# A new order of the first microseconds: x ahead of half of W's second piece, and gamma and b_up spread behind the first half product

## The reference

```python
h = jnp.einsum('bsh,bhk->bsk', hidden_states, W_down[role]) + b_down[role][:, None, :]
h = jax.nn.gelu(h, approximate=False)
u = jnp.einsum('bsk,bkh->bsh', h, W_up[role]) + b_up[role][:, None, :]
y = hidden_states + u
mean = jnp.mean(y, axis=-1, keepdims=True)
var = jnp.mean(jnp.square(y - mean), axis=-1, keepdims=True)
yn = (y - mean) * jax.lax.rsqrt(var + LN_EPS)
return yn * gamma[role][:, None, :] + beta[role][:, None, :]
```

## Time and profile before

| | |
|---|---|
| median of 3 runs | 1417.29 us (1417.27 to 1417.34) |
| the profiled execution | 1416.96 us |
| its span | 1415.2 us |
| PE busy | 1401.1 us, 99% |
| DVE busy | 1204.8 us, 85% |
| ACT busy | 776.8 us, 55% |
| first product on PE | 12.17 us after the start of the span |

### The profile page before, as it was taken

One profiled execution on the slowest core, in us unless ns is written; L12 is line 12 of the kernel. 1 busy time (PEld: TensorE's weight loads), 2 busy tenths in 40 slices (PEclk: granted clock), 3 DMA queues, 4 the chain that ended last, 5 costly groups with the idle time before them and its releaser, 6 DMA issues.

```text
span 1415.2 us, 29331 instructions
## 1 busy us (share of the span) xinstructions
PE 1401.1 (99%) x6175; PEld 1158.2 (82%) x6176; DVE 1204.8 (85%) x1458; ACT 776.8 (55%) x2047; POOL 201.0 (14%) x300
## 2 busy tenths in 40 slices
PE   8999999999999999999999999999999999999997
PEld 6888888888888888888888888888888888888886
DVE  8798988888888888888888899988888888888887
ACT  5555555555555555555555555555555555555555
POOL 4376311100000000000000377311100000000000
PEclk9999999999999999999999999999999999999999
DMA  8677777766566666665666778777765666656654
GB/s 230 183 225 241 215 212 200 211 195 198 184 195 199 194 184 196 200 192 184 194 200 193 213 227 234 222 198 201 218 199 185 196 200 190 185 194 199 192 186 149
DMA packets 208868, 283.49 MB, mean 200 GB/s; under 512 B 25791, under 2 KB 155584, under 8 KB 208846
## 3 DMA queue, kind: packets, MB, share of 16 engines
q1 hardware_dynamic: 201438, 269.34, 61.4%
q0 software_dynamic: 5888, 12.07, 4.6%
q10 hardware_dynamic: 1520, 1.84, 0.4%
HBM read 183.27 MB, written 99.88 MB: 200 GB/s over the span
## 4 chain that ended last, share of the span: by engine, by line
PE 98%; DVE 1%; DMA 1%; issue 0%; ACT 0%; DVEq 0%; ACTq 0%
PE p_up L1120 16%; PE p_up L1118 16%; PE p_up L1119 16%; PE p_down L1118 16%; PE p_down L1120 16%; PE p_down L1119 16%; DMA row<-in_L_cond_W_down 0%; DMA x_quad<-in_x 0%; DVE row L1038 0%; PE p_hT L1114 0%; DVE row L866 0%; DMA w_raw<-in_itok_B 0%; DVE x_quad L820 0%; DVE wd_lo L758 0%; DVE x_quad L1024 0%
## 5 line engine op out<-in xcount | busy, mean ns | idle before, releaser
L1118 PE MATMUL p_down<-wd_hi,xT_hi 128*128 x1012 | 393.9, 389 | 0.7 <-DVE xT_lo L782 0.4
L1120 PE MATMUL p_down<-wd_hi,xT_lo 128*128 x1012 | 393.7, 389 | 0.0
L1119 PE MATMUL p_down<-wd_lo,xT_hi 128*128 x1012 | 393.7, 389 | 0.0
L1118 PE MATMUL p_up<-wu_hi,hT_hi 128*128 x1008 | 392.3, 389 | 0.0
L1120 PE MATMUL p_up<-wu_hi,hT_lo 128*128 x1008 | 392.1, 389 | 0.0
L1119 PE MATMUL p_up<-wu_lo,hT_hi 128*128 x1008 | 392.1, 389 | 0.0
L595 ACT ACTIVATE hT_hi<-p_hT 128x512 fp32r<-128x512 f32 x126 | 75.7, 601 | 381.5 <-DVE p_hT L800 378.9
L820 DVE SCALAR_TENSOR_TENSOR row<-p_up,row 128x1024 f32<-128x1024 f32 x126 | 154.2, 1224 | 126.3 <-PE p_up L1120 126.2
L581 ACT ACTIVATE xT_hi<-xT_raw 128x1024 fp32r<-128x1024 f32 x125 | 132.8, 1062 | 187.6 <-PE p_down L1120 185.6
L1118 PEld LDWEIGHTS p_down<-wd_hi,xT_hi 128*128 128x128 f32 x1012 | 189.6, 187 | 40.8 <-issue 1.4
L1119 PEld LDWEIGHTS p_down<-wd_lo,xT_hi 128*128 128x128 f32 x1012 | 190.3, 188 | 39.7
(11 more groups left out here) (174 smaller groups left out, 981.3 us busy)
## 6 DMA issues: line engine op xcount, KB each, us to landing
x_quad<-in_x SPq DMA_DIRECT2D x510, 128.0 KB, 3.4
row<-in_x SPq DMA_DIRECT2D x126, 512.0 KB, 4.0
out<-row SPq DMA_DIRECT2D x126, 512.0 KB, 2.7
h_dram<-h SPq DMA_DIRECT2D x125, 256.0 KB, 4.1
h_quad<-h_dram SPq DMA_DIRECT2D x498, 64.0 KB, 1.9
w_raw<-in_L_cond_W_down POOLq DMA_DIRECT2D x64, 64.0 KB, 3.2
w_raw<-in_L_cond_W_up POOLq DMA_DIRECT2D x64, 64.0 KB, 3.6
row<-in_L_cond_W_up SPq DMA_DIRECT2D x16, 128.0 KB, 3.6
```

Source lines behind the costliest of these rows:

```text
L1118: pe.matmul(dst, a_hi, w_hi, start=first, stop=False)
L1119: pe.matmul(dst, a_hi, w_lo, start=False, stop=False)
L1120: return pe.matmul(dst, a_lo, w_hi, start=False, stop=last)
```

## The change

In the order of the engines' functions:

- SP: one register load of four item numbers in place of two single ones. x of item 0 (quarters 0 and 1), then quarters 2 and 3 of W's piece 1, then x of item 1, then all of piece 2, then piece 3. Before: x of item 0 (0 and 1), x of item 1, half of piece 2, piece 3.
- ACT: issues only quarters 0 and 1 of piece 1 at the start, rounds piece 0, and issues quarters 2 and 3 of item 0's x behind that. It rounds the parameter rows (DVE did). The first half of item 0's x is rounded ahead of piece 1. The half of piece 2 that it issued is gone. b_down's copy stands behind item 0's second half.
- POOL: no memset of zeros; a wait asks for the identity too.
- DVE: the selector is made ahead of the item order; the identity is made later; other order of the transposes, subtractions and splits.
- PE: no matmuls on zeros; five `keep_clock` in place of two, and none behind the spreading; gamma and b_up (four matmuls) are spread behind the first half product; `half_product` waits for each part (high of x, low of W, low of x) only where it needs it, and the order of its matmuls is by part.

```diff
@@ SP
             sp.wait_ge(first_known, 1)
-            for b, quads in ((0, range(0, NQ // 2)), (1, range(NQ))):
-                load_quads(sp, sp.value_load(first_numbers[0:1, b:b + 1], min_val=0, max_val=B - 1), b, quads)
-            load_first(sp, FD - 2, range(NQ // 2, NQ))
+            sp.load(number_reg, first_numbers[0:1, 0:RING])
+            load_quads(sp, sp.snap(number_reg[0], min_val=0, max_val=B - 1), 0, range(0, NQ // 2))
+            load_first(sp, 1, range(NQ // 2, NQ))
+            load_quads(sp, sp.snap(number_reg[1], min_val=0, max_val=B - 1), 1)
+            load_first(sp, FD - 2)
             load_first(sp, FD - 1)
@@ ACT
-            load_first(act, 1)
-            act.wait_ge(first_known, 1)
-            load_quads(act, act.value_load(first_numbers[0:1, 0:1], min_val=0, max_val=B - 1), 0, range(NQ // 2, NQ))
+            load_first(act, 1, range(0, NQ // 2))
...
+            round_first(0)
...
+            act.wait_ge(first_known, 1)
+            act.load(number_reg, first_numbers[0:1, 0:RING])
+            load_quads(act, act.snap(number_reg[0], min_val=0, max_val=B - 1), 0, range(NQ // 2, NQ))
+            act.wait_ge(param_rows_loaded, 16 * 8)
+            act.activation(rows, rows_raw, ACT.Copy).then_inc(param_rows_hi, 1)
...
-            round_first(0)
             act.wait_ge(order_in_psum, 1)
             act.activation(table[0:1, NUMBER:NUMBER + B], p_up[0][0:1, 2 * B:3 * B], ACT.Copy).then_inc(numbers_ready, 1)
+            round_half(0, 0)
             round_first(1)
-            round_half(0, 0)
-            load_first(act, FD - 2, range(0, NQ // 2))
             copy_param(2, p_up[1][:, :], BETA, H, beta_loaded)
-            copy_param(1, p_hT[:, :], BD, K, bias_loaded)
             round_half(1, 0)
             round_half(0, 1)
+            copy_param(1, p_hT[:, :], BD, K, bias_loaded)
@@ DVE
-            dve.wait_ge(param_rows_loaded, 16 * 8)
-            dve.tensor_copy(rows, rows_raw).then_inc(param_rows_hi, 1)
...
             transpose_half(0, 0)
+            transpose_half(0, 1)
+            subtract_half(0, 0)
+            dve.tensor_scalar(ident, index_row, number_col[:, :], None, ALU.is_equal).then_inc(ident_ready, 1)
             split_chunk(1, 0, chunk_split)
-            subtract_half(0, 0)
+            transpose_half(1, 0)
             split_chunk(1, 1, first_split)
-            transpose_half(1, 0)
-            transpose_half(0, 1)
             subtract_half(1, 0)
             subtract_half(0, 1)
-            transpose_half(1, 1)
             split_first(2)
             split_first(3)
+            transpose_half(1, 1)
             subtract_half(1, 1)
@@ PE
-            pe.wait_ge(zeros_ready, 1)
-            for _ in range(2):
-                mm = pe.matmul(p_down[:, :], xT_lo[:, 0, :], xT_lo[:, 0:HALF, :], start=True, stop=True)
-            mm.then_inc(zeros_used, 1)
             pe.wait_ge(first_hi, 1)
-            keep_clock(2)
-            pe.wait_ge(ident_ready, 2)
+            keep_clock(5)
+            pe.wait_ge(ident_ready, 1)
             pe.wait_ge(param_rows_split, 1)
             spread(p_hT[:, :], 0).then_inc(params_spread, 1)
             spread(p_up[1][:, 0:512], 1)
             spread(p_up[1][:, 512:H], 2).then_inc(params_spread, 1)
-            spread(p_sq[:, 0:512], 3)
-            spread(p_sq[:, 512:H], 4).then_inc(params_spread, 1)
-            pe.wait_ge(numbers_ready, 1)
-            spread(p_up[0][:, 0:512], 5)
-            spread(p_up[0][:, 512:H], 6).then_inc(params_spread, 1)
-            keep_clock(1)
-            pe.wait_ge(half_hi, 1)
-            keep_clock(1)
@@ PE, half_product of item 0 (items 1 and 2: four hi x hi, four hi x lo, a wait, four lo x hi)
+                pe.wait_ge(x_hi, b + 1)
...
+                early, rest = chunks[0:2], chunks[2:4]
+                piece = first // 2
+                pe.wait_ge(first_hi, piece + 1)
+                for c in early:
+                    hi_by_hi(c)
+                pe.wait_ge(first_split, piece + 1)
+                for c in early:
+                    hi_by_lo(c)
+                pe.wait_ge(x_lo, 1)
+                for c in early:
+                    lo_by_hi(c)
+                pe.wait_ge(first_hi, piece + 2)
+                for c in rest:
+                    hi_by_hi(c)
+                for c in rest:
+                    lo_by_hi(c)
+                if half == 0:
+                    pe.wait_ge(chunk_split, 1)
+                    hi_by_lo(rest[0])
+                pe.wait_ge(first_split, piece + 2)
+                for c in rest[1 - half:]:
+                    mm = hi_by_lo(c, c == HC - 1)
@@ PE, after the first half product
             half_product(0, 0, p_down[:, :], weights_at[0]).then_inc(half_down, 1)
+            spread(p_sq[:, 0:512], 3)
+            spread(p_sq[:, 512:H], 4).then_inc(params_spread, 1)
+            pe.wait_ge(numbers_ready, 1)
+            spread(p_up[0][:, 0:512], 5)
+            spread(p_up[0][:, 512:H], 6).then_inc(params_spread, 1)
```

More of the change, by code:

```diff
@@ L308, in load_x @@
                 load_quads(sp, n, b % 2)
+            number_reg = [sp.alloc_register(f"first_number{n}") for n in range(RING)]
             sp.wait_ge(first_known, 1)
-            for b, quads in ((0, range(0, NQ // 2)), (1, range(NQ))):
-                load_quads(sp, sp.value_load(first_numbers[0:1, b:b + 1], min_val=0, max_val=B - 1), b, quads)
-            load_first(sp, FD - 2, range(NQ // 2, NQ))
+            sp.load(number_reg, first_numbers[0:1, 0:RING])
[3 more added lines that the diff above has]
+            load_first(sp, FD - 2)
             load_first(sp, FD - 1)
@@ L398, in _ @@
             pool.memset(opener[:, 0:2], 0.0).then_inc(pieces_split, 1)
-            pool.memset(xT_lo[:, 0:HALF, :].bitcast(F32), 0.0).then_inc(zeros_ready, 1)
             done = [0]
@@ L470, in _ @@
             pool.wait_ge(numbers_ready, 1)
-            pool.wait_ge(ident_ready, 1)
+            pool.wait_ge(ident_ready, 2)
             pool.wait_ge(params_spread, 4)
@@ L558, in round_first @@
                 act.activation(hi, buf, ACT.Copy).then_inc(first_hi, 1)
+            round_first(0)
+            number_reg = [act.alloc_register(f"first_number{n}") for n in range(RING)]
+            act.wait_ge(first_known, 1)
[3 more added lines that the diff above has]
+            act.activation(rows, rows_raw, ACT.Copy).then_inc(param_rows_hi, 1)
             def copy_param(n, src, at, size, loaded):
@@ L752, in _ @@
                               ALU.is_equal).then_inc(ident_ready, 1)
-            dve.tensor_scalar(ident, index_row, number_col[:, :], None, ALU.is_equal).then_inc(ident_ready, 1)
+            dve.wait_ge(key_spread, 1)
+            chain(dve.tensor_copy(key_col[:, :], p_up[0][:, B:B + 1]))
+            chain(dve.tensor_scalar(onehot, p_up[0][:, 0:B], key_col[:, :], None, ALU.is_gt, ALU.add, accum_out=rank[:, :]))
+            dve.tensor_scalar(onehot, index_row, rank[:, :], None, ALU.is_equal).then_inc(order_ready, 1)
             def split_first(n):
@@ L1111, in turn_h @@
                 else:
+                    pe.wait_ge(ident_ready, 2)
                     pe.wait_ge(bias_loaded, 16)
@@ L1159, in half_product @@
                 hi, lo = half_x(b, half)
-                for c in range(half * HALF, half * HALF + HALF):
-                    if (b, c) == (0, FC // K):
-                        pe.wait_ge(chunk_split, 1)
-                    elif (b, c) == (0, FC // K + 1):
-                        pe.wait_ge(first_split, 2)
-                    elif b == 0 and c % (FC // K) == 0:
-                        pe.wait_ge(first_split, c // (FC // K) + 1)
-                    mm = product(dst, hi[:, c % HALF, :], lo[:, c % HALF, :], cols(wd_hi, at + c * K, K),
-                                 cols(wd_lo, at + c * K, K), c == 0, c == HC - 1)
+                first, last = half * HALF, half * HALF + HALF - 1
@@ new lines, in hi_by_hi, with hi_by_lo, lo_by_hi @@
+                def hi_by_hi(c):
+                    pe.matmul(dst, hi[:, c % HALF, :], cols(wd_hi, at + c * K, K), start=c == 0, stop=False)
+                def hi_by_lo(c, stop=False):
+                    return pe.matmul(dst, hi[:, c % HALF, :], cols(wd_lo, at + c * K, K), start=False, stop=stop)
+                def lo_by_hi(c, stop=False):
+                    return pe.matmul(dst, lo[:, c % HALF, :], cols(wd_hi, at + c * K, K), start=False, stop=stop)
+                chunks = range(first, last + 1)
@@ new lines, in half_product @@
+                x_hi, x_lo = (half_hi, half_lo) if half == 0 else (x_hi_ready, x_lo_ready)
+                pe.wait_ge(x_hi, b + 1)
+                if b > 0:
+                    for c in chunks:
+                        hi_by_hi(c)
+                    for c in chunks:
+                        hi_by_lo(c)
+                    pe.wait_ge(x_lo, b + 1)
+                    for c in chunks:
+                        mm = lo_by_hi(c, c == HC - 1)
+                    return mm
```

(1 more changed line is left out.)

22 lines of the change are left out of this document (6 added, 16 removed).

## The result

| | before | after |
|---|---|---|
| median (22 runs each) | 1417.36 us | 1419.47 us |
| lowest and highest | 1417.13, 1418.14 | 1418.86, 1420.64 |
| ratio of after to before | | 1.0015 (95% interval 1.0009 to 1.0021) |
| profiled execution, span | 1416.96, 1415.2 | 1418.92, 1417.2 |
| item 0's h turned on PE at | 23.75 | 25.44 |

The forecast was 1419.0 with a range of 1416.9 to 1420.2. The difference is within 0.2%, but its interval excludes no change. The runs of after also lie further apart: 1.8 us, against 1.0 before; the profiled execution is one of the lowest.

What follows compares the result with a forecast made beforehand. PE, busy 99% of the span, was taken to bound the kernel. The h side's +1.7 at the turning of item 0's h, other edits at nothing, gave 1417.29 + 1.7 = 1419.0 us; 8-in-10 range 1416.9 to 1420.2.

Steps and rivals of the forecast that it cites:

- What decides: Item 0's h turned on PE: the later of PE and the h side sets it, 25.45 instead of 23.75, +1.7.
- The h side: ACT and DVE from W's piece 3 landing (17.3) to item 0's gelu (25.45); sets the turning, +1.7, chance 0.60.
- ACT's issue of x: ACT's queue: its two quarters of item 0's x issued at about 6.6 and 7.15, one microsecond later than before.
- the landing: Item 0's last x quarter: lands between 9.75 and 10.75, taken as 10.1.
- The estimate worked out by it, 10.4: DMA engines taking turns between queue rows: x lands near 10.4, PE's own sum +0.5, hidden by the h side.
- PE's own sum: PE starts at 11.6, reaches the turning at 23.95, 0.2 later; rival that PE sets it: 0 to +1.0, chance 0.22.
- The stop in the first half product: PE's last matmul there waits for the second low half of W's piece 1: 0.4, from nothing to 1.0.
- case D: Low array clock at the first products; if low until 19.5, turning at 27.2, +3.4, 1420.7; rival's chance 0.09.
- The argument: Against case D: granted clock 1.00 over 5 idle us at the end, so a 1.7 us gap doesn't lower it.
- The price: Case D: 0.2 more for each slow product; the stop of 0.4 and wait of 1.5 swallow the first nine.
- No change on the chip's scale: Whole kernel: within 0.2% (2.83 us) of before, chance 0.92; slower 0.07, faster 0.01.

Runs made afterwards that it cites:

- e3: The changed kernel with the edits of e1 and e2 together (x issued before the rounding, transpose put back): 1417.67 us.
- e1: The changed kernel with ACT issuing its two quarters of item 0's x before it rounds W's piece 0: 1418.56 us.
- e6: The changed kernel with the edits of e1, e2 and e4 together: 1417.75 us.
- e7: e6 with all four quarters of W's second piece issued by ACT at the start, none by SP: 1416.70 us.
- c0: The changed kernel with a register clamp wherever a number loaded from memory is waited for; all follow-up runs carry these clamps: 1419.58 us.
- e4: The changed kernel with gamma and b_up spread ahead of the first half product again, behind the other three spreads: 1419.24 us.
- e2: The changed kernel with DVE's transpose of item 1's second half put back ahead of the splits of W's pieces 2 and 3: 1419.82 us.
- e9: The changed kernel with five more matmuls whose result isn't used, behind the three spreads ahead of the first product: 1419.09 us.
- e5: The changed kernel with only ACT issuing all four quarters of W's second piece at the start, SP none: 1419.48 us.
- e11: e7 with three keeping matmuls in place of five: 1418.41 us.

## Why the prediction was right, point by point

**What decides: right.** The turning of item 0's h was named as the place where both sides meet, and behind it all but 0.27 keeps its distance. After turned it at 25.44; the forecast was 25.45.

**The h side: right, term by term.** Piece 3 was forecast to land at 17.3 and landed at 17.4; split done 19.7 and 19.77; transposed 20.35 and 20.38; both copies done 22.85 and 22.89; gelu 25.45 and 25.39. e3 against e1 shows that the transpose's place was nearly half of the loss (0.9), and e6 against e7 that piece 3 comes 1.2 earlier when ACT issues the two quarters at the start.

**ACT's issue of x: right in the issue, wrong in the landing.** The issues stood at 6.53 and about 7.03 (forecast 6.6 and 7.15). The term that was mis-sized is the landing: 10.1 forecast, 10.75 its bound, 11.06 measured, that is 4.0 after the issue (4.6 in c0) where the earlier trace rows had 3.6 with more W ahead. SP had issued x, x, W, W before and beside it and went on at one each 0.5. The Trainium skill's page "DMA: Bandwidth & Descriptors", section on queues, rings and completion order, has the engines take turns between queue rows. A second queue's transfers sharing with the first's backlog would be later, and the trace agrees in direction, but no run here shows that it was this. The estimate worked out by it, 10.4, was too early as well.

**PE's own sum: wrong by 0.9.** It started at 12.67, not 11.6. Its last matmul ahead of the turning began at 24.64, so it could have turned h at 24.87 (forecast 23.95), and it lost 0.57 there (0.41 of it idle) and not 1.5. The stop in the first half product was priced at 0.4 and was 0.15, since a PE that starts late meets W's low part ready; with x early it was 0.77 (e3). That the time came out near was therefore partly luck: had the h side been 0.6 earlier, PE would have set the turning at +1.1, where the forecast's sum for PE said +0.2. For the same reason e1's 1.6 at the start moved the turning by only 0.2, and the spreading (e4) buys little alone.

**The clock, case D: mechanism right, its argument against beside the point, its chance too low.** The argument was that 5 idle us at the end leave the granted clock at 1.00, so that a short gap does not lower a clock that is up. In c0 it wasn't up: the spreads ahead of the gap and the products behind it both stood 0.43 apart. And where it was up the argument failed too: in e2 the clock had been full, the array idled for 2.37 up to 12.63, and from 13.4 on the products ran at half. 5 of the 22 runs of after lie over 1420.3, and e9, which fills the gap, has none there. The price was taken rightly: 0.2 for each slow matmul, less what PE would wait anyway (e1). The forecast's 1419.0 lacks 0.47. The clock is part of it: it was worth 0.5 in c0's median (e9), but without its five highest runs after's median is still 1419.34. The 0.27 behind the turning is of a like size; how the two share isn't known. The Trainium skill's "TensorE: Matmul & The Clock Gate", Part 1, has the half clock as the state of an idle array. I gave case D 0.09; by their times 5 of 22 runs of after and 5 of 11 of c0 are of that kind, of which one was profiled.

**No change on the chip's scale: right.** Within 0.2%, and the sign was right.

## What to carry to other kernels

Where two chains meet at one step, write down both arrival times and the room between them: an edit on one chain alone moves the step by no more than that room (0.2 in e1, whose time gained more by other ways), and two edits that seem to be worth 1.0 and nothing can be worth 1.9 together (e1, e2, e3). A rounding that is moved ahead of two transfers in a queue looks free on its engine; here its wait for W put x's issue one microsecond back. Two transfers fewer ahead of a lull let the transfers run dry (DMA share 0.61 in e6, 1.02 in e7), and all that follows lands later. Here it paid to keep the array working up to the products (e9), but with work that ends before they could start: in e6 it delayed them to 12.7, where e3 started at 11.0.

## What the runs showed of the hardware that I had not expected

- In e2 the array's clock fell near the start, after a stretch with little work (0.26 of 2.6 us busy; full before, half from 13.4 to 16.7), while it stayed full over 5 us with 0.11 of work at the end of before.
- The profile's clock column reads 1.00 until the clock's first rise (c0: 1.00 from 13.4 to 16.7, with matmuls 0.43 apart). At the start the distance of the matmuls tells the level.
- The same kernel starts its products at either level from run to run. Where PE has no room behind it the runs form two groups (c0: 1419.1 to 1419.6 and 1420.4 to 1421.1, their middles 1.4 apart; e5: 2.1 apart). With five more matmuls whose result isn't used, ahead of the products, there is one (e9).
- Two keeping matmuls less ahead of the products made the kernel slower by 1.7 us (e11 against e7).
- What is late next: with the turning near 23.8 the chain of item 3's x shows. In e3 DVE sat idle for 1.42 until x's transfer had landed, its work on that x and then a bias that PE waits for (35.00 to 35.68) came behind, and PE began item 3's product 0.26 late (35.43 to 35.92 where 0.23 is the step), so further gains at the start would be partly lost there.
